# A two-layer transformer step on one core: the square roots of the second and the fourth norm in one GpSimd chain, the fourth norm's last part 48 steps later, and a new table of places

## The reference

```
h = layernorm(x) * (1 + ca) + sa;  x = x + ga * attention(h)          # norm 1 ("a")
h = layernorm(x) * (1 + cb) + sb;  x = x + gb * experts(h)            # norm 2 ("b")
h = layernorm(x) * (1 + ca) + sa;  x = x + ga * state_space(h)        # norm 3 ("n", "s")
h = layernorm(x) * (1 + cb) + sb;  x = x + gb * tanh(h @ W + bias)    # norm 4 ("f")
layernorm(x) = (x - mean) / sqrt(var + 1e-5)
```

## Time and profile before

| | us |
|---|---|
| median of 3 runs | 2553.65 |
| lowest, highest | 2543.91, 2556.72 |
| the profiled execution's own time | 2561.15 |
| its span, first to last instruction | 2559.3 |
| busy: TensorE, VectorE, ScalarE, GpSimd | 2092.2, 1875.0, 1627.8, 1696.5 |

### The profile page before, as it was taken

How to read it: one execution, slowest core, us unless ns; L and a number is a source line. 1 busy time by engine, 2 the same in 40 slices (tenths; PEclk the granted TensorE clock), 3 DMA queues, 4 the chain that set the end, 5 groups by cost and what they waited for, 6 DMA issues and landing times. The chain is left out here.

```text
span 2559.3 us, 41613 instructions
## 1 busy us (share of the span) xinstructions
PE 2092.2 (82%) x11705; PEld 973.9 (38%) x11840; DVE 1875.0 (73%) x3194; ACT 1627.8 (64%) x4159; POOL 1696.5 (66%) x2028
## 2 busy tenths in 40 slices
PE   4779988989898888989898888989898887868442
PEld 2444444434444344434444443434344443323110
DVE  2544668787777868787786878787786778768886
ACT  3655666767676666667676766667676666644442
POOL 1012259686877858686876969686876768687553
PEclk9889999999999999999999999999999999979665
DMA  7735396677768677767858677767758676545442
GB/s 145 102 59 106 66 185 129 142 148 161 133 128 160 125 147 133 151 139 153 150 112 162 126 160 137 152 139 155 152 107 166 121 145 132 119 105 145 108 131 59
DMA packets 534879, 338.83 MB, mean 132 GB/s; under 512 B 353929, under 2 KB 453177, under 8 KB 534201
## 3 DMA queue, kind: packets, MB, share of 16 engines
q1 hardware_dynamic: 534652, 336.16, 65.5%
HBM read 242.21 MB, written 26.74 MB: 105 GB/s over the span
## 5 line engine op out<-in xcount | busy, mean ns | idle before, releaser
L1301 POOL TENSOR_TENSOR work<-work,bc 128x512 f32<-128x512 f32 x512 | 657.8, 1293 | 164.5 <-PE bank L1337 131.5
L1307 DVE TENSOR_TENSOR_SCAN work<-bank,work 128x512 f32<-128x512 f32 x512 | 622.4, 1216 | 165.3 <-POOL work L1301 113.5
L1314 POOL TENSOR_TENSOR work<-work,bc 128x512 f32<-128x512 f32 x436 | 566.8, 1306 | 71.5 <-DVE work L1307 71.0
L1031 POOL TENSOR_TENSOR zh<-zh,w_bc 128x512 f32<-128x512 f32 x256 | 334.4, 1306 | 393.5 <-DVE zh L1024 393.2
L1290 ACT ACTIVATE bank<-work,neg_a 128x510 f32<-128x510 f32 x512 | 354.1, 692 | 292.4 <-DVE work L1307 275.7
L698 ACT ACTIVATE probs<-bank,nmax 128x256 f32<-128x256 f32 x1024 | 477.1, 479 | 27.3 <-DVE nmax L688 25.5
L688 DVE TENSOR_REDUCE nmax<-bank 128x2 f32<-128x512 f32 x512 | 334.6, 675 | 140.3 <-PE bank L680 140.0
L680 PE MATMUL bank<-ke,q_all 64*64 64x256 f32 x4096 | 300.2, 411 | 83.3 <-DVE zh L1024 63.0
L708 PEld LDWEIGHTS bank<-ident,probs 128*128 128x128 f32 x2048 | 254.7, 145 | 290.9 <-issue 195.6
L708 PE MATMUL bank<-ident,probs 128*128 128x128 f32 x2048 | 322.4, 281 | 29.9 <-ACT probs_t L716 29.2
L716 ACT ACTIVATE probs_t<-bank 128x512 f32<-128x512 f32 x512 | 304.9, 595 | 65.7 <-PE bank L708 51.2
(11 more groups left out here) (187 smaller groups left out, 2406.3 us busy)
## 6 DMA issues: line engine op xcount, KB each, us to landing
work<-dt_rows SPq DMA_DIRECT2D x256, 512.0 KB, 6.0
ke<-low SPq DMA_DIRECT2D x256, 256.0 KB, 6.0
w_bc<-w_rows_d SPq DMA_DIRECT2D x256, 256.0 KB, 4.6
q_all<-q_rows SPq DMA_DIRECT2D x1024, 8.0 KB
bc<-bc_rows SPq DMA_DIRECT2D x64, 256.0 KB, 6.4
x_in<-in_x SPq DMA_DIRECT2D x32, 256.0 KB, 4.8
dt_rows<-step SPq DMA_DIRECT2D x16, 512.0 KB, 3.0
dt_rows<-step SPq DMA_DIRECT2D x32, 256.0 KB, 3.4
```

What stands on the lines that cost most here:

```text
L1031: nc.gpsimd.tensor_tensor(zh[:, n % 3, :], zh[:, n % 3, :], w_bc[:, n % WB, :], ALU.mult).then_inc(m_p, 1)
L1301: nc.gpsimd.tensor_tensor(hb[at % HB], ring[n % RING][:, 1, :], bc[:, s, :], ALU.mult).then_inc(s_dbx, 1)
L1307: nc.vector.tensor_tensor_scan(hb[at % HB], decay_bank(p, m)[:, :], hb[at % HB], 0.0, ALU.mult, ALU.add).then_inc(s_h, 1)
L1314: nc.gpsimd.tensor_tensor(hb[at % HB], hb[at % HB], bc[:, SG + batch(m)[2], :], ALU.mult).then_inc(s_hc, 1)
```

## The change

Norms 2 and 4 get common root buffers (`ROOT_BF`, eight columns). Up to pair 11 the root of norm 4 of pair u is computed in the chain of norm 2 of pair u + 3; the last four pairs' norm 4 keeps chains of its own, of eight columns as well, as has norm 2 of pair 15. Each chain now waits for both norms' inputs and for both norms' earlier results to have been used. The last part from f_norm on moves later by 18 to 49 steps (f_norm from 524 to 542, f_turned from 526 to 574, f_end from 530 to 577, the store from 538 to 575), so that it stands between the router's weights and the end of the experts. Two waits follow from sharing the bank in the new place. Most other places move by a few steps, and the tables for the last pairs have a fourth entry.

```diff
-        S_LATE = 3
+        S_LATE, F_LATE = 3, 3
         ROOT_AS = root_buffers("as", 2 * TILES)
         LN_A = ln_buffers("a", xn_a, a_h, ROOT_AS, 0)
-        LN_B = ln_buffers("b", xn_b, b_h)
+        ROOT_BF = root_buffers("bf", 2 * TILES)
+        LN_B = ln_buffers("b", xn_b, b_h, ROOT_BF, 0)
         LN_S = ln_buffers("n", xn_s, n_h, ROOT_AS, 1, S_LATE)
-        LN_F = ln_buffers("f", xn_s, f_h)
+        LN_F = ln_buffers("f", xn_s, f_h, ROOT_BF, 1, F_LATE)
...
-            f_turned_tensor=526, f_mix_tensor=527, s_decay_scalar=-1, m_tanh_scalar=3,
...
+            f_back_tensor=511, f_turned_tensor=574, f_mix_tensor=576, s_decay_scalar=-1,
...
-        def ln_root_gpsimd(pool, L, p):
-            pool.wait_ge(L["s_mv"], p + 1)
-            if p:
-                pool.wait_ge(L["s_xn"], p)
-            root_gpsimd(pool, L["root"], p)
+        MERGED = PAIRS - 4
...
+        def f_root_of(u):
+            return u + F_LATE if u < MERGED else MERGED + F_LATE + own_roots().index(place("f_root_gpsimd", u))
...
+        def bf_root_gpsimd(pool, b, f):
+
+            q = b_root_of(b) if b is not None else f_root_of(f)
+            b_before, f_before = (sum(root_of(u) < q for u in range(PAIRS)) for root_of in (b_root_of, f_root_of))
+            if f is not None:
+                pool.wait_ge(LN_F["s_mv"], f + 1)
+            if f_before:
+                pool.wait_ge(LN_F["s_xn"], f_before)
+            if b is not None:
+                pool.wait_ge(LN_B["s_mv"], b + 1)
+            if b_before:
+                pool.wait_ge(LN_B["s_xn"], b_before)
+            root_gpsimd(pool, ROOT_BF, q)
...
             if g == 1 and p:
                 pe.wait_ge(m_cp, p)
+                ended = before("f_end_tensor", GROUP_STEPS * n + AT["a_values_tensor"])
+                if ended:
+                    pe.wait_ge(f_x, ended)
...
             pe.wait_ge(a_on, groups_valued(place("f_turned_tensor", p)))
+            pe.wait_ge(m_cp, before("m_weights_tensor", place("f_turned_tensor", p)))
             ln_tensor(pe, LN_F, bank[3], p)
```

More of the change, by code:

```diff
@@ new lines, in build @@
+                a_end_vector=149, m_route_vector=[163, 166, 170, 173, 173, 173, 175, 177, 177, 177,
+                178, 178, 178, 178, 180, 180, 181, 181, 181, 181], m_end_vector=281,
+                s_stats_vector=284, s_conv_vector=[[300, 301, 302, 306], [317, 317, 317, 317]],
+                s_silu_vector=[313, 318], s_step_vector=[330, 331], s_zgate_vector=[411, 418],
+                s_end_vector=[423, 475], f_res_vector=511, f_stats_vector=527, s_root_gpsimd=288,
+                f_root_gpsimd=484, f_end_vector=530, m_logits_scalar=164,
@@ L353, in build @@
-                f_res_vector=504, f_stats_vector=504, f_end_vector=534, s_root_gpsimd=309,
-                f_root_gpsimd=512,
+                s_rows_sync=353, s_rows_in_sync=[362, 365, 363, 369], s_store_sync=[350, 355],
+                a_back_tensor=151, b_turned_tensor=160, m_weights_tensor=184, m_back_tensor=303,
+                s_turned_tensor=320, s_in_x_tensor=[328, 332], s_step_tensor=[343, 345],
+                s_rows_tensor=350, s_in_z_tensor=[390, 392], f_out_tensor=495, f_back_tensor=502,
@@ L358, in build @@
[L358 to L362, removed]
+                f_store_sync=531, a_back_tensor=149, b_turned_tensor=158, m_weights_tensor=186,
@@ new lines, in build @@
+                s_rows_tensor=372, f_out_tensor=505, f_turned_tensor=526, f_end_tensor=531,
+                b_turned_scalar=162, m_weights_scalar=187, m_end_scalar=323, s_norm_scalar=333,
+                f_out_scalar=510, f_turned_scalar=523, f_norm_scalar=520, a_end_vector=151,
+                s_silu_vector=[353, 364], s_step_vector=[369, 373], s_end_vector=[451, 501],
+                f_stats_vector=514, f_back_tensor=511, f_res_vector=511, f_root_gpsimd=518,
+                f_mix_tensor=528, f_mix_scalar=531, f_end_vector=533, s_zgate_vector=[387, 398],
@@ new lines, in build @@
+                s_step_tensor=[363, 366], s_turned_tensor=338, s_turned_scalar=341,
+                b_norm_scalar=158, m_end_vector=325, s_stats_vector=326,
+            ),
+            4: dict(
+                f_out_tensor=507, f_out_scalar=509, f_back_tensor=509, f_res_vector=511,
+                f_stats_vector=512, f_root_gpsimd=516, f_norm_scalar=523, f_turned_tensor=523,
+                f_turned_scalar=524, f_mix_tensor=525, f_mix_scalar=526, f_end_tensor=530,
+                f_end_vector=532, f_store_sync=532, m_back_tensor=325, m_end_scalar=323,
+                m_logits_tensor=162, s_stats_vector=327, s_rows_scalar=376, m_weights_tensor=186,
@@ L491, in ln_stats_vector, with own_roots, b_root_of, bf_roots_due @@
             last.then_inc(L["s_mv"], 1)
-        def ln_root_gpsimd(pool, L, p):
-            pool.wait_ge(L["s_mv"], p + 1)
-            if p:
-                pool.wait_ge(L["s_xn"], p)
-            root_gpsimd(pool, L["root"], p)
+        MERGED = PAIRS - 4
+        def own_roots():
+            by_b = [place("b_root_gpsimd", u) for u in range(MERGED + F_LATE, PAIRS)]
+            by_f = [place("f_root_gpsimd", u) for u in range(MERGED, PAIRS)]
+            return sorted(set(by_b + by_f))
+        def b_root_of(u):
+            return u if u < MERGED + F_LATE else MERGED + F_LATE + own_roots().index(place("b_root_gpsimd", u))
+        def f_root_of(u):
+            return u + F_LATE if u < MERGED else MERGED + F_LATE + own_roots().index(place("f_root_gpsimd", u))
+        def bf_roots_due(st):
+            b = next((u for u in range(PAIRS) if place("b_root_gpsimd", u) == st), None)
+            f = next((u for u in range(PAIRS) if (place("f_root_gpsimd", u) if u >= MERGED else place("b_root_gpsimd", u + F_LATE)) == st), None)
+            return b, f
+        def bf_root_gpsimd(pool, b, f):
[10 more added lines that the diff above has]
+            root_gpsimd(pool, ROOT_BF, q)
         def as_root_gpsimd(pool, q):
@@ L533, in ln_norm_scalar @@
         def ln_norm_scalar(act, L, x, p):
-            act.wait_ge(L["s_rstd"], p + L["late"] + 1)
+            act.wait_ge(L["s_rstd"], (f_root_of(p) if L is LN_F else b_root_of(p) if L is LN_B else p + L["late"]) + 1)
             for t in range(TILES):
```

118 lines of the change are left out of this document (54 added, 64 removed).

## The result

| | us |
|---|---|
| median now (4 runs) | 2460.07 |
| lowest, highest | 2453.88, 2462.11 |
| before, in the same runs | 2555.18 |
| ratio, 95% interval | 0.9632 [0.9604, 0.966] |
| the profiled execution's own time, its span | 2462.11, 2460.3 |

The account below looks back on a forecast made before the run. No engine is full; engines waiting for each other in turn set a pair's period. 3.4 less 2.2 plus 1.1 is 2.3 us per pair, with three more second norms 31 us, so 2523 from the median; range 2485 to 2564.

Parts of the forecast that it names:

- Steps (1) and (2): Fourth norm's old stretch: freed root chain (0 to 4.43 us) and departing last part together save 3.4 us per pair.
- Step (3): Routing stretch: the last part's arrival makes VectorE wait about 1.8 us and add 0.69; 2.2 us per pair lost.
- Step (4): Second norm: its transposes now stand behind the scores, which fill part of TensorE's 3.19 us wait; 1.1 us saved.
- Step (5): All other table places, mostly moved one to four steps, and the last four pairs: taken as 0.
- my three signs of being wrong: VectorE waiting for the store ahead of m_end_vector; routing over 3 us per pair longer; last 439 us changed by over 10.
- More than summed: Rival: four engines get lighter in one stretch; 4.4, 0.7, 1.1 plus 1.7 of clock, 6.5 per pair, 2475; chance 0.17.
- Slack: Rival: GpSimd's freed time was slack and the last part's waits only change place; 2543 to 2560 us; chance 0.17.
- The store's wait: Rival: m_end_vector waits for the output store to land, 4.7 us in each of 12 pairs, 2578 us; chance 0.12.

Follow-up runs that it names:

- move only: The changed kernel with every steady-pair place but the fourth norm's last part's back at its old number; 2509.56 us, ratio 0.9809.
- chain at the old place: The changed kernel plus 16 unused GpSimd root instructions where norm 4's root stood, in each of 12 pairs; 2487.79 us, ratio 0.9727.
- turn early: The changed kernel with the second norm's transposes back ahead of the scores (b_turned_tensor 160 to 158); 2474.69 us, ratio 0.9682.
- last tables: The kernel before with the changed place tables of its last three pairs, all else as before; 2549.43 us, ratio 0.9962.
- places only: The kernel before with the changed steady-pair places, except the fourth norm's root and last part and the attention output product's; 2507.52 us, ratio 0.9809.
- chain at the new place: The changed kernel plus 16 unused GpSimd root instructions directly ahead of the joint root, in each of 12 pairs; 2526.85 us, ratio 0.9882.

## Why the prediction was wrong, step by step

*Steps (1) and (2), root and last part leave: 3.4 per pair, measured 3.5* (move only, slots 8 to 10). Right, and by the mechanism: the chain's own share is 2.0 of its 4.43 us (chain at the old place), between my bounds. The rest, the last part's work and waits, was not divided further. With the new places the same move gives 4.2 there (27.92 against 23.71).

*Step (3), the last part enters the routing: 2.2 lost, measured 0.1 gained with the old places and 1.9 lost with the new ones* (27.52 against 25.63). This step failed for the move. I laid scores, f_mix, tanh, scaling and transposes one behind the other and took VectorE to be there 1.8 us early. By my own rows the five are 4.45 us, from 994.5 on they end at 998.95 and not at 999.5, and the wait would have been 1.3. In move only, it does the two z gate multiplications (2.2 us) and the inverse's diagonal first, and the addition stands with no wait:

```profile
983.47 0.91 ACT L1471 ACTIVATE y_x<-y_x,mod 128x256 f32<-128x256 f32 x2
...
984.54 1.00 DVE L819 TENSOR_TENSOR dg<-rinv,mask_d 128x512 f32<-128x512 f32 x1
985.47 0.67 DVE L1481 TENSOR_TENSOR x_b<-x_b,bank 128x512 f32<-128x512 f32 x1
```

And where it does wait (now, 1.1 us), ending the wait gave nothing.

*Step (4), the transposes behind the scores: 1.1, measured 1.6* (turn early). The size was near by luck, and the mechanism failed. I priced the part of the wait that the scores fill and said of the clock "I take nothing". The pair of turn early that keeps the full clock through a wait of 3.24 us is as fast as the pairs are now, so the fill was worth 0 there, and the 1.6 are the clock's: it fell in two of nine pairs now, in seven of the eight that wait 3.3 us in turn early and in all nine before. Per 3.4 us at 0.50 it cost 1.3, where I had named at most 1.7. By the Trainium skill, page "TensorE: Matmul & The Clock Gate", section "HAM oscillation", a kernel that waits again and again between bursts pays a second time in slow matmuls. This pair of runs agrees, with 1.3 and 2.5 us where the clock fell and 0 where it did not.

*Step (5), everything else 0: measured half of the gain.* This is the step that put the result outside the range. It was not worked out but waved through: "Most places move by one to four steps." In an in-order program one step is one place in a queue, and by reversal the routing's places, the convolution's and SyncE's transfers' decide over 2.5 to 3.2 us per pair each, the norms' over 1.0. Beyond the steady pairs I took 0 as well; the last tables gave 10 us (last tables), and places only began pair 3's experts 9 us earlier (551.8 for 561.1). The last stretch, 24 us shorter, is the one of my three signs of being wrong that came true; VectorE does not wait for the store, and slots 14 to 0 are not longer.

*The rivals.* "More than summed" is what happened, in its size (2475, measured 2460), but its reasons were half of it: 3.5 and not 4.4 at the old place, 0 and not 0.7 at the new one, and of its 1.1 and 1.7 behind the second norm 1.6 came, the clock's; it knew nothing of the places. Its 2475 was also taken from the profiled execution: from the median its 86 us give 2468, and half of them 2511, not 2500. "Slack" fell: the chain costs 2.0 at the old place. The store's wait fell at its condition: it needed a landing of 6.5 us, and the stores land in 2.3. The page "Perfetto Trace Analysis" of the Trainium skill, section "Identifying the Most-Contended Engine", would have one optimize the engine with the highest occupancy first. That time on another engine is then worth nothing, as I read it for this rival, is not borne out: GpSimd is third by occupancy (66%), and 16 small instructions more per pair on it cost 24 us at one place and 64 at the other (by the ratios, 0.9727 and 0.9882 against 0.9632).

## What to carry over

In a kernel whose order is written out step by step, go through the order of every engine and of the DMA queue before a table of small numbers is priced at nothing; half of this gain was there. A freed or added stretch of time has no price of its own: 4.4 us cost 2.0 or 5.3 by what waits behind them. And price a fitted table as a whole, since its parts by reversal add up to three times the whole, and a part alone may give nothing. Where a wait lets the clock fall, look for a pair in which it did not: it tells what the wait costs without the clock.

## What I had not expected of the hardware

The longer the wait ahead of the second norm's transposes, the more of a pair ran at 0.50: 0.8 us per pair with a wait of 1.7 us, 4.2 with 3.3, and 8.7 with 6.3 (now, turn early, chain at the new place). But the same wait does not always do the same: of eight pairs with 3.3 us the clock fell in seven, and of nine with 1.7 in two. Summed over the nine steady pairs the clock stood at 0.50 for 58 us before and 7 now.

The same 256 KB output store lands in 7.3 us in the median at the old place, and in 2.3 at the new one. No run moved the store alone.
